# A gated block over 64 sequences: outputs read back by groups, a normalisation ahead of a copy, a wide split ahead of an exponent

## The chip, the cores and the metric

The kernel runs on one core of one Trainium2 chip, in one launch. The time is that of the device in microseconds. Five engines work side by side, each through its own list of instructions, and meet through semaphores: PE (TensorE) multiplies matrices, DVE (VectorE) and POOL (GpSimd) work elementwise on SBUF, DVE on PSUM too, ACT (ScalarE) applies functions, and SP issues DMAs, as ACT does for some.

## The reference

Each of 64 sequences has 256 rows of 512 features, all float32. In short:

```
def xattn(q, k, v, w, b):                    # 16 heads of 32 features
    q, k, v = relu(q), relu(k), relu(v)
    att = softmax(q k^T / sqrt(32))          # 256 x 256 for each head
    return relu(att v @ w.T + b)

def ffn(x, W_r, W_k, W_v, mu_r, mu_k):
    x_prev = x shifted down by one row
    r = sigmoid((mu_r * x + (1 - mu_r) * x_prev) @ W_r)
    k = (mu_k * x + (1 - mu_k) * x_prev) @ W_k
    return r * (relu(k) ** 2 @ W_v)

x = x + tanh(g_xattn) * xattn(layernorm(x), ctx, ctx, w, b)
x = x + tanh(g_ffn) * ffn(layernorm(x), W_r, W_k, W_v, mu_r, mu_k)
```

## The kernel before

**Tiling.** A sequence b has two row tiles u of 128 rows, four feature chunks of 128, and 16 heads n in CH = 4 groups c of GR = 4. Float32 operands of the large products are split into a high and a low part (`q_high`, `k_low`, `o_high`, `o_low`, `xk_high`, `xk_low` and so on), and a product is three matmuls of such parts. ACT makes high parts, DVE or POOL the low ones.

**Attention.** Scores of a head are computed twice. PE makes `scores` (L1084) in one of two banks, `s_bank[n % 2]`; DVE takes each row's maximum, `head_max` (L855). For a group, PE turns the four heads' maxima (L1059), DVE copies them, `copy_m` (L864), and SP moves them by DMA into one row of the stacked queries, `move_m` (L300). PE then makes `shifted_scores` (L1096), in which that row subtracts the maximum, ACT applies `exponent` (L616), and PE sums with the values (L1110) and with ones (L1122, the denominators). For group 1 the denominators come another way: ACT's `sum_exp` (L628) applies the exponential to the first scores of heads 4 to 7 in their bank and accumulates the sum. A later head's `scores` needs the bank back: those of head 7 wait until `sum_exp` of head 5 is done, those of head 10 for `head_max` of head 8.

**Output of attention.** `norm_o` (L877 reciprocal, L879 multiply) writes group c into `o_val[c % 2]`. SP writes it to DRAM, `write_o` (L307), in a transposing layout, and reads a row tile's two groups back as `o_mv` when both are written, `read_o` (L316: 4 DMAs of 64 KB each). ACT copies it out as the high part, `o_high` (L637), POOL makes the low one, `o_low` (L429), and PE projects (L1139, `w_hi,o_hi`). `o_mv` is one buffer, reused by each row tile: it may be overwritten when `o_lo` of the tile before is done. In the kernel before this is guarded by a wait in `norm_o` of the odd groups.

**Second half.** `add_x`, the second layernorm, a turn on PE, the differences between rows (POOL L438) and the mixes `mix_k` (L923) and `mix_r` (L932, four instructions that add to `xd` in place) feed key, value and receptance; `ka_square` (POOL L462) squares the key. `finish` multiplies by the gate (L940: th) and adds to x (L943: x1), which SP stores (L323). `load_x1` on ACT (L534) loads the next x into that buffer, once the store is done.

**Order.** The work is a software pipeline: iteration i holds, interleaved, the first layernorm of sequence i+2, the attention of i and i+1, and the second halves of i-1 to i-3. Each engine has a list of its own for an iteration, written out by hand; iterations -3 to 3 and 60 to 66 are unrolled, the 56 between run as a hardware loop of pairs. Nothing reorders the lists: an instruction that waits holds up all behind it on its engine. The names that follow are those of the rows: `o_hi<-o_mv` is `o_high`, `bank<-bank,m_nat` `sum_exp`, `probs<-bank` `exponent`, `k_raw<-k_raw,k_high` `k_low` (L844, in place), `xk_lo<-xm,xk_hi` `xk_low` (L447), `q_st<-q_dram` `stack_q` (L578, L579), `q_dram<-q_raw` a part of `write_q` (L568), `k_st<-k_dram` `stack_k`.

SP's list of an iteration before, at its start and where tile 0 is read:

```
stack_k(i, 3, par); store(i - 3, 1 - par); move_m(i, 1); write_o(i - 1, 3); read_o(i - 1, 1)
...
load_x(i + 3); move_m(i, 3); write_o(i, 1); stack_k(i + 1, 2, 1 - par); move_m(i + 1, 0); read_o(i, 0)
```

Of the kernel before, what the change touches and what calls it, by code (L numbers as in the profile page):

```python
# [16 lines left out]
def flamingo_block(nc, x, ctx_in, ctx_t, g_xattn, g_ffn, w_t, bias, mu, out):  # L17
# [19 lines left out]
    HD = D // HEADS  # L37
    NU = T // P
# [9 lines left out]
    with es:  # L48
# [119 lines left out]
        o_moved = sem("o_moved")  # L168
# [68 lines left out]
        def _(sp):  # L237
# [71 lines left out]
            def read_o(b, u):  # L309

                if on(b):

                    for half in o_written:
                        sp.wait_ge(half, 16 * (2 * b + u + 1))
                    for m in range(GR):
                        sp.dma_start(o_mv[HD * m:HD * m + HD, :, :],  # L316
                                     o_dram[2 * u:2 * u + 2, :, :, m, :].rearrange("c g f r -> f (c g) r")
                                     ).then_inc(o_moved, 16)
# [12 lines left out]
            def opening(i, par):  # L331
# [6 lines left out]
                elif i == -1:  # L338
                    stack_k(0, 0, 1 - par)
                    stack_k(0, 1, 1 - par)  # L340
                    load_k(1)
                    move_m(0, 0)
                    stack_k(0, 2, 1 - par)
                    load_x(2)
                else:
                    stack_k(0, 3, par)
                    move_m(0, 1)
                    load_w(range(4, 5))
                    write_k(1, 1 - par)
                    move_m(0, 2)  # L350
                    load_w(range(5, 6))
                    keys_written(1)
                    stack_k(1, 0, 1 - par)
                    load_k(2)
                    move_m(0, 3)
                    load_w(range(6, 7))
                    write_o(0, 0)
                    stack_k(1, 1, 1 - par)
                    load_x(3)
                    write_o(0, 1)  # L360
                    stack_k(1, 2, 1 - par)
                    move_m(1, 0)
                    load_w(range(7, 8))
                    read_o(0, 0)
                    write_k(2, par)
                    write_o(0, 2)

            def iteration(i, par):
# [3 lines left out]
                stack_k(i, 3, par)  # L372
                if isinstance(i, int) and i == NB + 2:
                    store_last(i - 3, 1 - par)
                else:
                    store(i - 3, 1 - par)
                move_m(i, 1)
                write_o(i - 1, 3)
                read_o(i - 1, 1)
# [6 lines left out]
                load_x(i + 3)  # L386
                move_m(i, 3)
                write_o(i, 1)
                stack_k(i + 1, 2, 1 - par)
                move_m(i + 1, 0)  # L390
                read_o(i, 0)
# [105 lines left out]
        def _(act):  # L497
# [135 lines left out]
            def o_high(b, u):  # L633
                if on(b):
                    act.wait_ge(o_moved, 16 * GR * (NU * b + u + 1))
# [66 lines left out]
            def iteration(i, par):  # L702
                stack_q(i, 3, par)
                if isinstance(i, int) and i == NB + 1:
                    xr_high(i - 2)
                exponent(i, 0)
                sum_exp(i, 6)
# [72 lines left out]
                exponent(i, 15)  # L780
                sum_exp(i + 1, 5)
                o_high(i, 0)
# [5 lines left out]
        def _(dve):  # L788
# [77 lines left out]
            def norm_o(b, c):  # L866
                if on(b):
# [3 lines left out]
                    if c % 2 == 1:  # L871

                        after(dve, o_lo_ready, NU * b + c // 2)
# [62 lines left out]
            def finish(b, u, par):  # L936
                if on(b):
# [3 lines left out]
                                                   in1=dense_bank[u][:, :], op0=ALU.add, op1=ALU.mult).then_inc(y_ready, 1)  # L941
                    dve.wait_ge(y_ready, NU * b + u + 1)
# [3 lines left out]
            def iteration(i, par):  # L946

                head_max(i, 7)
                halve_gate(i)
                finish(i - 3, 1, 1 - par)  # L950
                copy_m(i, 1)
                norm_o(i - 1, 3)
# [52 lines left out]
                head_max(i + 1, 4)  # L1005
                finish(i - 2, 0, par)
# [363 lines left out]
```

## Time and profile before

| | us |
|---|---|
| median of 3 runs | 2733.62 |
| lowest and highest | 2730.46, 2733.77 |
| profiled execution, its own time | 2731.21 |
| its span | 2729.4 |
| PE busy | 2656.8 (97%) |
| DVE busy | 2298.1 (84%) |
| ACT busy | 1693.1 (62%) |
| POOL busy | 1100.4 (40%) |
| mean granted TensorE clock | 0.988 |

The DMA engines moved 576.74 MB, 211 GB/s over the span. The busy digits of PE are 9 (90% or more) in 37 of the 40 slices; only the first two and the last are below. The share of an engine says how much of the span it computed. With PE at 97%, the time is PE's work and its waits; what another engine does counts only where PE, or something that ends in PE, waits for it. The profiled execution's time is some 1.8 us above its span: what lies around the program.

### The profile page before, as it was taken

How to read it: one execution, taken by the hardware profiler on the slowest of the kernel's cores; microseconds unless marked ns; L12 is line 12 of the kernel's file. 1: busy time of each engine (PE TensorE's matmuls, PEld its weight loads, DVE VectorE, ACT ScalarE, POOL GpSimd, SP SyncE). 2: the span in 40 equal slices, each digit the busy share in tenths (PEclk: the TensorE clock that was granted, in tenths of full speed). 3: DMA queues.
4: the chain of work that ended last, by engine and by line, in shares of the span. 5: the costliest groups of instructions: out<-in, count | busy, mean ns of one | idle time of the engine just before them, and what ended most of it. 6: DMA issues, size and time to landing. Idle time of an engine off the chain costs nothing. (4 is left out here: it accounts for less than half of the span.)

```text
span 2729.4 us, 66171 instructions
## 1 busy us (share of the span) xinstructions
PE 2656.8 (97%) x20354; PEld 2061.7 (76%) x20354; DVE 2298.1 (84%) x4109; ACT 1693.1 (62%) x3531; POOL 1100.4 (40%) x902
## 2 busy tenths in 40 slices
PE   4899999999999999999999999999999999999998
PEld 2677777777777777777777777777777777777776
DVE  6777888888888888888888888888888888888775
ACT  4555666666666666666666666666666666666553
POOL 0243444444444444444444444444444444444434
PEclk9799999999999999999999999999999999999999
DMA  8877778777778778778778778778778778778641
GB/s 252 231 190 213 216 205 231 219 204 231 218 205 231 217 205 233 217 205 233 215 205 235 214 205 235 212 206 237 212 206 236 211 206 234 214 208 232 183 145 45
DMA packets 515023, 576.74 MB, mean 211 GB/s; under 512 B 183072, under 2 KB 414496, under 8 KB 514976
## 3 DMA queue, kind: packets, MB, share of 16 engines
q1 hardware_dynamic: 361456, 340.68, 45.6%
q10 hardware_dynamic: 153520, 235.46, 29.0%
q8 instruction: 26, 0.43, 0.1%
q14 instruction: 21, 0.17, 0.0%
HBM read 373.56 MB, written 201.33 MB: 211 GB/s over the span
## 5 line engine op out<-in xcount | busy, mean ns | idle before, releaser
L616 ACT ACTIVATE probs<-bank 128x512 f32<-128x512 f32 x1024 | 604.2, 596 | 527.8 <-PE bank L1096 477.4
L855 DVE TENSOR_REDUCE m_nat<-bank 128x2 fp32r<-128x512 f32 x1024 | 687.1, 681 | 90.0 <-PE bank L1084 89.8
L1084 PE MATMUL bank<-k_st,q_st 96*128 96x256 f32 x2048 | 439.3, 297 | 18.1 <-ACT bank L628 6.8
L1096 PE MATMUL bank<-q_st,k_st 97*128 97x256 f32 x2048 | 427.0, 290 | 4.9 <-DMA q_st<-m_t 4.5
L1096 PEld LDWEIGHTS bank<-q_st,k_st 97*128 97x128 f32 x2048 | 358.7, 192 | 84.1 <-issue 27.1
L1084 PEld LDWEIGHTS bank<-k_st,q_st 96*128 96x128 f32 x2048 | 360.7, 194 | 81.0 <-ACT bank L628 17.9
L877 DVE RECIPROCAL o_val<-bank 128x256 f32<-128x256 f32 x192 | 336.2, 1751 | 62.6 <-PE bank L1122 59.7
L429 POOL TENSOR_TENSOR o_lo<-o_mv,o_hi 128x512 fp32r<-128x512 f32 x128 | 166.7, 1302 | 444.3 <-ACT o_hi L637 436.1
L628 ACT ACTIVATE bank<-bank,m_nat 128x256 f32<-128x256 f32 x512 | 227.5, 444 | 186.6 <-DVE m_nat L855 186.6
L462 POOL TENSOR_TENSOR xm<-xm 128x512 f32<-128x512 f32 x128 | 133.8, 1045 | 408.0 <-ACT xm L674 408.0
L1139 PE MATMUL bank<-xk_hi,w_hi 128*128 128x256 f32 x1024 | 296.5, 290 | 1.0 <-DVE th L940 1.0
L1139 PE MATMUL bank<-xk_hi,w_lo 128*128 128x256 f32 x1024 | 288.2, 281 | 0.0
L1139 PE MATMUL bank<-xk_lo,w_hi 128*128 128x256 f32 x1024 | 287.9, 281 | 0.0
L1110 PE MATMUL bank<-probs,v_pos 128*32 128x256 f32 x4096 | 278.2, 390 | 0.0
L421 POOL TENSOR_TENSOR rstd<-ve,mhalf 128x1 f32<-128x1 f32 x128 | 69.2, 541 | 456.4 <-DVE ve L907 456.4
L1139 PE MATMUL bank<-w_hi,o_hi 128*128 128x512 f32 x512 | 212.8, 416 | 14.0 <-POOL o_lo L429 13.8
L447 POOL TENSOR_TENSOR xk_lo<-xm,xk_hi 128x512 fp32r<-128x512 f32 x128 | 172.9, 1351 | 128.4 <-DVE xm L923 111.6
L1139 PEld LDWEIGHTS bank<-xk_hi,w_hi 128*128 128x128 f32 x1024 | 192.5, 188 | 27.4 <-issue 25.9
L864 DVE CAST m_t<-bank 8x128 fp32r<-8x128 f32 x256 | 70.9, 277 | 168.6 <-PE bank L1059 168.2
L1139 PE MATMUL bank<-w_hi,ka_hi 128*128 128x512 f32 x512 | 209.1, 408 | 0.0
L1122 PE MATMUL bank<-probs,ones_r 128*32 128x256 f32 x3072 | 209.0, 390 | 0.0
L1139 PE MATMUL bank<-w_hi,xr_hi 128*128 128x512 f32 x512 | 208.0, 406 | 0.0
(94 smaller groups left out, 6088.3 us busy)
## 6 DMA issues: line engine op xcount, KB each, us to landing
q_st<-q_dram ACTq DMA_DIRECT2D x256, 256.0 KB, 4.8
k_st<-k_dram SPq DMA_DIRECT2D x256, 256.0 KB, 4.3
k_raw<-ctx_t_dram SPq DMA_DIRECT2D x256, 128.0 KB, 4.9
q_st<-q_dram ACTq DMA_DIRECT2D x256, 128.0 KB, 2.5
k_st<-k_dram SPq DMA_DIRECT2D x256, 128.0 KB, 4.8
o_dram<-o_val SPq DMA_DIRECT2D x256, 128.0 KB, 2.2
o_mv<-o_dram SPq DMA_DIRECT2D x512, 64.0 KB, 2.1
x<-x_dram ACTq DMA_DIRECT2D x64, 512.0 KB, 6.4
```

What stands on the lines that cost most here:

```text
L429: nc.gpsimd.tensor_tensor(by_tile(o_lo, u), o_mv[:, :, :].rearrange("p g (k a) -> p k g a", k=KC), by_tile(o_hi, u).bitcast(F32), ALU.subt ...
L447: nc.gpsimd.tensor_tensor(xk_lo[:, part, :], xm[:, part, :], xk_hi[:, part, :].bitcast(F32), ALU.subtract).then_inc(xk_lo_ready, 1)
L462: nc.gpsimd.tensor_tensor(part, part, part, ALU.mult).then_inc(ka_ready, 1)
L616: nc.scalar.activation(probs[:, n // GR % 2, n % GR, :, :].rearrange("p v t -> p (v t)"), st_bank[n % 2][:, :], ACT.Exp).then_inc(exp_read ...
L628: last = nc.scalar.activation(scores, scores, ACT.Exp, bias=m_nat[:, SUMMED % 2, g, u:u + 1].bitcast(F32), accum_out=den[:, NU * g + u:NU ...
L855: nc.vector.tensor_reduce(m_nat[:, c % 2, n % GR, :], s_bank[n % 2][:, :].rearrange("p (u y) -> p u y", u=NU), AX_X, ALU.max, negate=True) ...
L877: nc.vector.reciprocal(o_val[:, c % 2, :], pv_bank[:, T:2 * T]).then_inc(rden_ready, 1)
L1084: mm = nc.tensor.matmul(s_bank[n % 2][:, T * u:T * u + T], q_st[0:QK, c, g, P * u:P * u + P], k_st[0:QK, c, g, :], start=True, stop=True)
L1096: mm = nc.tensor.matmul(st_bank[n % 2][:, T * v:T * v + T], k_st[0:ST, c, g, P * v:P * v + P], q_st[0:ST, c, g, :], start=True, stop=True)
L1110: nc.tensor.matmul(pv_bank[HD * g:HD * g + HD, 0:T], v_pos[:, v, HD * h:HD * h + HD], probs[:, c % 2, g, v, :], start=(v == 0), stop=(v == ...
L1122: mm = nc.tensor.matmul(pv_bank[HD * g:HD * g + HD, T:2 * T], ones_r[:, 0:HD].bitcast(F32), moving, start=(n == 0), stop=(n == len(sums) - 1))
L1139: mm = nc.tensor.matmul(dst, lhs[a], rhs[c], start=first and n == 0, stop=last and n == 2, skip_group_check=True)
```

## The change

It has three parts.

- **Reads by halves.** `o_moved` becomes two semaphores. `read_o(b, u, half)` waits for the low part of the tile before (this guard moves here from `norm_o`) and for the write of group 2u + half alone, and reads that group: 4 DMAs of 32 KB for each half. The first half of tile 0 is issued ahead of `move_m(i, 3)`, the second ahead of `move_m(i + 1, 0)` (both stood behind it); the first half of tile 1 stands ahead of the last group's write, the second behind the store. The store itself goes behind that write and `move_m(i, 1)`. `o_high` waits for both halves.
- **DVE.** `finish` becomes `gate` and `finish`. At an iteration's start `gate` and `norm_o` of the last group stand first, then `copy_m`, the rest of the finish, and `mix_r`.
- **ACT.** `o_high(i, 0)` stands ahead of `sum_exp(i + 1, 5)` rather than behind it, and `stack_q(i, 3)` behind `exponent(i, 0)` rather than ahead of it.

```diff
@@ -165,7 +165,7 @@
         rsum_spread = sem("rsum_spread")
         o_ready = sem("o_ready")
         o_written = [sem("o_written0"), sem("o_written1")]
-        o_moved = sem("o_moved")
+        o_moved = [sem("o_moved0"), sem("o_moved1")]
         o_hi_ready = sem("o_hi_ready")
         o_lo_ready = sem("o_lo_ready")
         z_ready = sem("z_ready")
@@ -306,16 +306,15 @@
                     sp.wait_ge(o_ready, CH * b + c + 1)
                     sp.dma_start(o_dram[c].rearrange("g f m r -> (g f) (m r)"), o_val[:, c % 2, :]).then_inc(o_written[c % 2], 16)

-            def read_o(b, u):
-
-                if on(b):
-
-                    for half in o_written:
-                        sp.wait_ge(half, 16 * (2 * b + u + 1))
+            def read_o(b, u, half):
+
+                if on(b):
+                    after(sp, o_lo_ready, NU * b + u)
+                    sp.wait_ge(o_written[half], 16 * (2 * b + u + 1))
                     for m in range(GR):
-                        sp.dma_start(o_mv[HD * m:HD * m + HD, :, :],
-                                     o_dram[2 * u:2 * u + 2, :, :, m, :].rearrange("c g f r -> f (c g) r")
-                                     ).then_inc(o_moved, 16)
+                        sp.dma_start(o_mv[HD * m:HD * m + HD, GR * half:GR * half + GR, :],
+                                     o_dram[2 * u + half, :, :, m, :].rearrange("g f r -> f g r")
+                                     ).then_inc(o_moved[half], 16)

             def store(b, par):
                 if on(b):
@@ -361,7 +360,8 @@
                     stack_k(1, 2, 1 - par)
                     move_m(1, 0)
                     load_w(range(7, 8))
-                    read_o(0, 0)
+                    read_o(0, 0, 0)
+                    read_o(0, 0, 1)
                     write_k(2, par)
                     write_o(0, 2)

@@ -370,13 +370,14 @@
                     opening(i, par)
                     return
                 stack_k(i, 3, par)
+                read_o(i - 1, 1, 0)
+                write_o(i - 1, 3)
+                move_m(i, 1)
                 if isinstance(i, int) and i == NB + 2:
                     store_last(i - 3, 1 - par)
                 else:
                     store(i - 3, 1 - par)
-                move_m(i, 1)
-                write_o(i - 1, 3)
-                read_o(i - 1, 1)
+                read_o(i - 1, 1, 1)
                 keys_written(i + 1)
                 stack_k(i + 1, 0, 1 - par)
                 load_k(i + 2)
@@ -384,11 +385,12 @@
                 write_o(i, 0)
                 stack_k(i + 1, 1, 1 - par)
                 load_x(i + 3)
+                read_o(i, 0, 0)
                 move_m(i, 3)
                 write_o(i, 1)
                 stack_k(i + 1, 2, 1 - par)
+                read_o(i, 0, 1)
                 move_m(i + 1, 0)
-                read_o(i, 0)
                 write_k(i + 2, par)
                 write_o(i, 2)

@@ -632,7 +634,8 @@

             def o_high(b, u):
                 if on(b):
-                    act.wait_ge(o_moved, 16 * GR * (NU * b + u + 1))
+                    for half in o_moved:
+                        act.wait_ge(half, 16 * GR * (NU * b + u + 1))
                     after(act, z_ready, NU * (b - 1) + u + 1)
                     nc.scalar.activation(by_tile(o_hi, u), o_mv[:, :, :].rearrange("p g (k a) -> p k g a", k=KC),
                                          ACT.Copy).then_inc(o_hi_ready, 1)
@@ -700,10 +703,10 @@
                                          scale=0.5).then_inc(th_ready, 1)

             def iteration(i, par):
-                stack_q(i, 3, par)
                 if isinstance(i, int) and i == NB + 1:
                     xr_high(i - 2)
                 exponent(i, 0)
+                stack_q(i, 3, par)
                 sum_exp(i, 6)

                 exponent(i, 1)
@@ -778,8 +781,8 @@
                 load_v(i + 1, 0)

                 exponent(i, 15)
+                o_high(i, 0)
                 sum_exp(i + 1, 5)
-                o_high(i, 0)

             pipeline(act, iteration)

@@ -868,9 +871,6 @@
                     dve.wait_ge(pv_ready, CH * b + c + 1)

                     after(dve, o_written[c % 2], 16 * (2 * b + c // 2))
-                    if c % 2 == 1:
-
-                        after(dve, o_lo_ready, NU * b + c // 2)
                     if c == SUMMED:
                         nc.vector.tensor_copy(o_val[:, c % 2, :], pv_bank[:, T:2 * T]).then_inc(rden_ready, 1)
                     else:
@@ -933,12 +933,15 @@
                                                               in1=xt[:, c, 0:T], op0=ALU.mult, op1=ALU.add)
                     last.then_inc(xr_ready, 1)

-            def finish(b, u, par):
+            def gate(b, u):
                 if on(b):
                     dve.wait_ge(vv_ready, NU * b + u + 1)
                     dve.wait_ge(th_ready, NU * b + u + 1)
                     nc.vector.scalar_tensor_tensor(out=th[:, u, :], in0=th[:, u, :], scalar=1.0,
                                                    in1=dense_bank[u][:, :], op0=ALU.add, op1=ALU.mult).then_inc(y_ready, 1)
+
+            def finish(b, u, par):
+                if on(b):
                     dve.wait_ge(y_ready, NU * b + u + 1)
                     nc.vector.scalar_tensor_tensor(out=x1[:, par, u, :], in0=th[:, u, :], scalar=tgh[:, 0:1],
                                                    in1=x1[:, par, u, :], op0=ALU.mult, op1=ALU.add).then_inc(out_ready, 1)
@@ -947,9 +950,10 @@

                 head_max(i, 7)
                 halve_gate(i)
+                gate(i - 3, 1)
+                norm_o(i - 1, 3)
+                copy_m(i, 1)
                 finish(i - 3, 1, 1 - par)
-                copy_m(i, 1)
-                norm_o(i - 1, 3)
                 if not (isinstance(i, int) and i == NB + 1):
                     mix_r(i - 2)

@@ -1003,6 +1007,7 @@
                 split_low(i, 4, 0)

                 head_max(i + 1, 4)
+                gate(i - 2, 0)
                 finish(i - 2, 0, par)

                 head_max(i + 1, 5)
```

ACT, at the boundary of two iterations inside the loop; `o_hi<-o_mv` is `o_high`, `bank,den<-bank,m_nat` the summed exponents (of head 5 above the branch of iterations, 6 and 7 behind), `q_st<-q_dram` the query stack. Before:

```order
L616 ACTIVATE probs<-bank 128x512
L622 REGISTER_ALU
L628 ACTIVATE bank,den<-bank,m_nat 128x256 x2
L635 ISA
L637 ACTIVATE o_hi<-o_mv 128x4x128
L578 DMA q_st<-q_dram 32x1024
L579 DMA q_st<-q_dram 64x1024
L609 REGISTER_ALU
L206 ISA
L616 ACTIVATE probs<-bank 128x512
```

After, in the same place:

```order
L618 ACTIVATE probs<-bank 128x512
L638 ISA
L640 ACTIVATE o_hi<-o_mv 128x4x128
L624 REGISTER_ALU
L630 ACTIVATE bank,den<-bank,m_nat 128x256 x2
L611 REGISTER_ALU
L206 ISA
L618 ACTIVATE probs<-bank 128x512
L580 DMA q_st<-q_dram 32x1024
L581 DMA q_st<-q_dram 64x1024
```

The high part of the output went ahead of head 5's summed exponent, and the two query DMAs behind the next exponent.

DVE, at the start of an iteration in the loop, behind the maxima of head 7: `th` is the gate, `x` the finish, `m_t` the copy of maxima, `o_val` the normalisation, `xd` the last mix. Before:

```order
L938 ISA
L940 SCALAR_TENSOR_TENSOR th<-th,bank 128x512
L943 SCALAR_TENSOR_TENSOR x<-th,tgh,x 128x512
L861 ISA
L206 ISA
L864 CAST m_t<-bank 8x128
L868 ISA
L206 ISA
L877 RECIPROCAL o_val<-bank 128x256
L879 TENSOR_TENSOR o_val<-bank,o_val 128x256
L932 SCALAR_TENSOR_TENSOR xd<-xd,mu_sb,xt 128x256 x4
```

After:

```order
L938 ISA
L940 SCALAR_TENSOR_TENSOR th<-th,bank 128x512
L871 ISA
L206 ISA
L877 RECIPROCAL o_val<-bank 128x256
L879 TENSOR_TENSOR o_val<-bank,o_val 128x256
L864 ISA
L206 ISA
L867 CAST m_t<-bank 8x128
L946 SCALAR_TENSOR_TENSOR x<-th,tgh,x 128x512
L932 SCALAR_TENSOR_TENSOR xd<-xd,mu_sb,xt 128x256 x4
```

The finish and the copy moved from ahead of the normalisation to behind it.

SP, from the key stack at the start of an iteration in the loop. Before:

```order
L291 DMA k_st<-k_dram 32x1024
L322 ISA
L323 ISA
L323 DMA out_dram<-x 128x2x512
L299 ISA
L300 DMA q_st<-m_t 1x8x128
L306 ISA
L307 DMA o_dram<-o_val 128x256
L314 ISA
L316 DMA o_mv<-o_dram 32x8x64 x4
```

After:

```order
L206 ISA
L313 ISA
L315 DMA o_mv<-o_dram 32x4x64 x4
L306 ISA
L307 DMA o_dram<-o_val 128x256
L299 ISA
L300 DMA q_st<-m_t 1x8x128
L321 ISA
L322 ISA
L322 DMA out_dram<-x 128x2x512
L315 DMA o_mv<-o_dram 32x4x64 x4
```

The write of the last group went ahead of the move of maxima and of the store; one half of the read stands ahead of all three, the other behind them.

## Rows read from the trace of the kernel before

**Rows 1.** Windows: start:end, us, busy of engines, granted clock, DMA share, GB/s

```profile
1319.22:1401.22 82.00, 81.86 (x638) 63.69 (x636) 71.32 (x129) 52.62 (x111) 34.48 (x28) 1.00 0.76 218
1975.22:2015.75 40.53, 40.53 (x319) 31.73 (x318) 34.90 (x65) 25.95 (x55) 17.08 (x14) 1.00 0.76 218
```

**Rows 2.** Timeline, a slow boundary and a quick one: start, us, engine, line, instruction

```profile
1319.38 0.20 ACT L628 ACTIVATION_READ_ACCUMULATOR bank<-bank,m_nat 128x1 f32 x1
1319.97 0.28 PE L1139 MATMUL bank<-xk_hi,w_hi 128*128 128x256 f32 x1
1321.89 0.08 PEld L1059 LDWEIGHTS bank<-ident_r,m_nat 128*8 128x8 f32 x1 [0.52 <-DVE m_nat L855]
...
1975.07 0.21 ACT L628 ACTIVATION_READ_ACCUMULATOR bank<-bank,m_nat 128x1 f32 x1
1975.70 0.28 PE L1139 MATMUL bank<-xk_hi,w_hi 128*128 128x256 f32 x1
```

**Rows 3.** Timeline, `xk_lo` on POOL and the keys on DVE, ahead of either boundary

```profile
1313.57 1.29 POOL L447 TENSOR_TENSOR xk_lo<-xm,xk_hi 128x512 fp32r<-128x512 f32 x1 [0.21 <-issue]
1313.78 2.16 DVE L844 SCALAR_TENSOR_TENSOR k_raw<-k_raw,k_high 128x1024 fp32r<-128x1024 f32 x1
...
1969.70 2.43 POOL L447 TENSOR_TENSOR xk_lo<-xm,xk_hi 128x512 fp32r<-128x512 f32 x1 [0.34 <-issue]
1969.78 1.20 DVE L844 SCALAR_TENSOR_TENSOR k_raw<-k_raw,k_high 128x1024 fp32r<-128x1024 f32 x1
```

**Rows 4.** Groups by line, L844: busy us, mean ns, idle before

```profile
L844 DVE SCALAR_TENSOR_TENSOR k_raw<-k_raw,k_high 128x1024 fp32r<-128x1024 f32 x64 | 125.8, 1966 | 0.0
```

**Rows 5.** Timeline, ACT's DMA issue of `q_raw`, ahead of either boundary

```profile
1312.12 0.53 ACTq L568 DMA_DIRECT2D q_dram<-q_raw  x1
...
1968.12 0.73 ACTq L568 DMA_DIRECT2D q_dram<-q_raw  x1
```

**Rows 6.** Waits, whole span: us in total, times, longest

```profile
PE bank L1139 <- POOL o_lo L429: 13.8, 7, 2.8
```

**Rows 7.** Windows, the longest of the disturbed iterations

```profile
206.01:252.39 46.38, 43.60 (x319) 34.02 (x318) 34.67 (x64) 26.26 (x57) 17.58 (x14) 0.93 0.71 198
```

**Rows 8.** Timeline, ACT, the other `o_high` of an iteration

```profile
1333.83 0.63 ACT L637 ACTIVATE o_hi<-o_mv 128x512 fp32r<-128x512 f32 x1 [1.83 <-DMA o_mv<-o_dram]
1334.37 0.58 ACT L616 ACTIVATE probs<-bank 128x512 f32<-128x512 f32 x1
```

**Rows 9.** Timeline, ACT, the first `o_high` of all

```profile
79.32 0.63 ACT L637 ACTIVATE o_hi<-o_mv 128x512 fp32r<-128x512 f32 x1 [4.43 <-DMA o_mv<-o_dram]
```

**Rows 10.** Timeline, DVE, POOL and PE behind the slow boundary

```profile
1322.47 0.75 DVE L943 SCALAR_TENSOR_TENSOR x<-th,tgh,x 128x512 f32<-128x512 f32 x1
1323.14 0.27 DVE L864 CAST m_t<-bank 8x128 fp32r<-8x128 f32 x1
1325.45 1.67 DVE L932 SCALAR_TENSOR_TENSOR xd<-xd,mu_sb,xt 128x256 f32<-128x256 f32 x4
1327.03 1.28 DVE L855 TENSOR_REDUCE m_nat<-bank 128x2 fp32r<-128x512 f32 x2
1327.36 1.04 POOL L462 TENSOR_TENSOR xm<-xm 128x512 f32<-128x512 f32 x1 [5.91 <-ACT xm L674]
1328.65 0.40 PE L1084 MATMUL bank<-k_st,q_st 96*128 96x256 f32 x2
```

**Rows 11.** Timeline, maxima moved and first used: steady, then in the start-up

```profile
1323.92 0.69 SPq L300 DMA_DIRECT2D q_st<-m_t  x1
1329.60 0.40 PE L1096 MATMUL bank<-q_st,k_st 97*128 97x256 f32 x2
...
43.02 0.69 SPq L300 DMA_DIRECT2D q_st<-m_t  x1
48.06 0.80 PE L1096 MATMUL bank<-q_st,k_st 97*128 97x256 f32 x2 [1.80 <-DMA q_st<-m_t]
```

**Rows 12.** The page, DMA issues: count, KB, us to landing

```profile
o_dram<-o_val SPq DMA_DIRECT2D x256, 128.0 KB, 2.2
```

## The prediction

> **What bounds the kernel now.** I read the windows first. Two stretches from the start of one iteration's first shifted product (sequence i+1, head 0) to a later one: two iterations in 82.00 us, 41.00 each, with PE busy for 81.86; and one of 40.53 us with PE busy for all of it [rows 1]. So PE sets the pace, and the 0.47 us between the two kinds is all that an ordinary iteration loses. The timeline at the boundary shows where. Scores of head 7 wait for ACT's summed exponent of head 5, which ends 0.36 us after the boundary in the slow kind (1319.38 + 0.20) and 0.06 after it in the quick kind; the dense product behind the scores starts at +0.75 and +0.48 [rows 2]. That is 0.27 of the 0.47. The other 0.2 follows at once, at the turn of the maxima, where PE waits for DVE.
>
> Why ACT is late is on DVE and POOL, six microseconds earlier. The scaling of keys (L844) takes 2.16 us where POOL's `xk_lo` record starts 0.21 us before it, and 1.20 us where it starts 0.08 before it; POOL's instruction is then the long one, 2.43 against 1.29 [rows 3]. Only one of the two proceeds at a time. All 64 of them take 125.8 us [rows 4]: with n long ones, 2.16n + 1.20(64 - n) = 125.8 gives 51 long and 13 short. Some 61 boundaries are steady ones, 51 slow and 10 quick. Where POOL's start slips, ACT's issue of `q_raw` took 0.73 us instead of 0.53 [rows 5]; it stands before the `xk_hi` that POOL waits for.
>
> Outside this, PE waits 13.8 us in 7 waits for POOL's `o_lo` [rows 6], in which `o_mv`, read back from DRAM, is late. The iteration with the longest takes 46.38 us at a mean granted clock of 0.93, so that part of it stands at the 1.2 GHz level behind the stall [rows 7]. Against 40.53 it loses 5.85, 2.1 times its wait of 2.8.
>
> **The change, part by part.**
> *`o_high` ahead of the summed exponent of head 5.* From `o_high` to the next ACT instruction is 1334.37 - 1333.83 = 0.54 us [rows 8], and now it stands on the very path that makes PE wait. In a slow iteration the dense product would start at +0.75 + 0.54 = 1.29, against 0.48 with no wait: 0.81 lost, and the second wait, for DVE at the turn, is covered by that. So 40.53 + 0.81 = 41.34, +0.34. In a quick iteration the exponent would end at 0.06 + 0.54 = 0.60; with the 0.39 us that the slow kind needs from its end to the dense product (0.75 - 0.36) that product starts at 0.99, a loss of 0.51: 41.04 us. Ten quick iterations: +5.1. Fifty-one slow ones that stay slow: +17.3; if they turn quick: 51 x 0.04 = +2.0. It also needs `o_mv` 0.6 us sooner, and in the start-up, where `o_high` waited 4.43 us for it with nothing behind [rows 9], the exponents and head 7's scores now wait too: about +3 once (bounds 0 and 4.4).
>
> *Does k_low win the port more often?* The change puts 128 KB of `o_mv` reads, which stood behind the move of the next maxima, ahead of it, so that they are in the queues when ACT issues `q_raw`. The quick kind needs a slip of POOL of only about 0.13 us (0.21 to 0.08), and the issue row moves by 0.20 when it moves [rows 3, 5]. I judge that it turns in 41 of the 51 (nearest rows: 10 of 61 now; bounds 0 and 51). Then 41 x 0.04 + 10 x 0.34 + 5.1 = +10.1 us for this and the part above; bounds +7.1 and +22.4.
>
> *Reads by halves.* Per row tile 256 KB still move, in 8 issues rather than 4 (SP has the idle time: its issues cost nothing on PE). Half 0 needs only group 2u, so it leaves early, and after the last group's write only 128 KB remain. The 7 waits are worth between 13.8 (the waits alone) and 13.8 x 2.1 = 29 us (with the lower clock behind each of them). The two or three short ones had no slow clock worth naming, so I take 24 for all and 20 of it as saved. Against it: in tile 1 the store of x (512 KB) now stands ahead of half 1 in SP's queue, so the saving could be 0.
>
> *DVE's start of the iteration.* Copy of the maxima (0.27) and the second part of the finish (0.75) go behind `norm_o`, which could not have started much earlier: it waits for PE's denominators. Between its multiply and `mix_r`, which started at 1325.45, stand the copy and the finish now: 0.67 from the finish's start to the next (1323.14 - 1322.47) and some 0.2 for the copy, less about 0.13 by which the reciprocal can start sooner than behind both. I take 0.74: `mix_r` at 1326.19. The maximum of head 8, which stood at 1327.03, moves to 1327.77 and ends some 0.65 later at 1328.42, and scores of head 10 on PE, its user, stand at 1328.65 [rows 10]. Slack 0.94 becomes 0.2: cost 0, with nothing to spare. The wait for `o_lo` that leaves `norm_o` cost nothing here, and goes to SP.
>
> *The maxima's move to `q_st`.* It was issued at 1323.92 and used at 1329.60, 5.7 us later. Now the copy ends at about 1325.8 and the issue follows at 1325.9: 3.7 us. One row speaks of it: in the start-up, issue at 43.02, product at 48.06 after a wait of 1.80 for this very move, 5.04 us [rows 11]; 128 KB of `o_dram` land in 2.2 [rows 12]. Bounds 0 and 1.34 us in each iteration. I take 0: the queue of the start-up was full of loads, and 2.2 is the row of the steady loop on that queue.
>
> *The store* leaves 3.5 us later, and with it the next x load on ACT, which is used ten microseconds on: 0, covered by PE. *Query stack behind exponent 0*: it takes off a 0.6 us issue gap before an exponent that PE does not wait for: 0 to -0.1 per iteration; I take 0.
>
> **Sum.** 2731.2 (the profiled execution) + 10.1 + 3 - 20 = 2724.3. The median of the runs shown, 2733.6, is 2.4 above the profiled one: 2726.7, say 2727.
>
> **Rivals.**
> 1. *The port race does not turn.* For it: 51 of 61 go POOL's way now. 2731.2 + 22.4 + 3 - 20 + 2.4 = 2739.0.
> 2. *`mix_r` loses the port to POOL's square* (the slower side). `ka_square` starts at 1327.36 and takes 1.04; `mix_r`'s last of four instructions would start at 1326.19 + 3 x 0.40 = 1327.4, at the same time. If POOL wins, the maximum of head 8 ends about 1 us later, the slack of 0.2 is gone, and PE waits 0.8 us for scores of head 10 in every iteration: 2726.7 + 61 x 0.8 = 2775. It decides from a POOL lead of about 0.1 to 0.2 us. Against it: the lead worked out is 0.0, and a slip of ACT moves POOL back, not forward.
> The Trainium skill, "SBUF — State Buffer", section "Who interferes with whom", says that the pair of ports shared by DVE and GpSimd is an exclusive lock that whoever starts first keeps for a whole instruction; a DVE instruction with two SBUF inputs contends with a reading GpSimd one. By that rule alone POOL, 0.04 ahead, would win here, and this rival would be the forecast. The trace agrees on the lock, but not to the tenth of a microsecond: in [rows 3] POOL's record starts 0.08 first, and it is POOL that waits.
> 3. *The reads of `o_mv` stay late*, dragged by the store ahead of them and the x load beside them: no saving of 20, 2746.7. For it: the store now shares their queue and their moment. Against: half of the bytes are gone by then.
> The Trainium skill, "DMA: Bandwidth & Descriptors", section "Queues, rings and completion order", has each DMA engine take packets of the queues in turns, and within a queue in ring order; by that the half behind the store has 512 KB before it and the x load beside it. No row of before shows that order.
> 4. *The move of maxima is late*: up to 1.34 us x 61, over 2800; half of that is likelier, 2765.
> 5. *More is gained*: all turn, the quicker start of exponent 0 hides half of `o_high`, and all 24 come off: about 2714.
>
> **Chances.** Forecast 0.42, its own range 2718 to 2733; rival 1 0.21; rival 2 0.12; rival 3 0.10; rival 4 0.05; rival 5 0.10. The range 2712 to 2760 leaves out most of rivals 2 and 4. A measurement tells about 0.2% (5.5 us) from no change. Faster (under 2728.1): 0.6 of the forecast and rival 5, 0.25 + 0.10, with a little of rival 1: 0.37. Slower (over 2739.1): half of rival 1, most of 3, all of 2 and 4: 0.11 + 0.08 + 0.17 = 0.36. Same: 0.27.
>
> **What would show it.** The count of long and short L844 (now 51 and 13): mostly short says that the race turned. The dense product at the boundary at about +0.99, and an iteration of 41.0 us where the race turned, 41.3 where not. No wait of PE for `o_lo` in the steady loop, and no iteration near 46 us. A wait of PE (L1084) for DVE's maximum nine microseconds after the boundary means rival 2, one at L1096 for the move of `m_t` rival 4. Wrong altogether if ordinary iterations fall below 40.9: then the 0.54 of `o_high` is not on the path as I have it.

## The result and the profile after

The change makes the kernel slower: 2742.85 us median of 6 runs (2739.48 to 2746.17) against 2732.04 of 6 (2721.71 to 2735.45), a ratio of 1.0046 with a 95% interval of 1.0026 to 1.0066. Forecast was 2727, a gain of 0.25%. The number lies inside the stated range; the sign is the other one. It is rival 1, the race for the port that does not turn, at 2739.0, and 4 us more. One run of e1 and two runs of the kernel before, at 3206, 5066 and 3656 us, were in a slow state and stand in none of the medians and ratios below.

The page after and, below it, the windows of the same 48 iterations before and after (start:end, us, busy time of each engine, granted clock, DMA share, GB/s):

```profile
span 2742.8 us, 66755 instructions
PE 2647.6 (97%) x20354; PEld 2053.6 (75%) x20354; DVE 2305.0 (84%) x4109; ACT 1687.2 (62%) x3531; POOL 1124.4 (41%) x902
```

```profile
376.67:2343.38 1966.71, 1963.67 (x15265) 1528.50 (x15264) 1712.20 (x3073) 1261.72 (x2641) 824.59 (x672) 1.00 0.77 218
```

```profile
372.71:2363.19 1990.48, 1965.43 (x15265) 1529.35 (x15264) 1720.55 (x3073) 1256.66 (x2641) 843.02 (x673) 1.00 0.79 215
```

Divided by 48: 40.97 us an iteration before, 41.47 after. These 48 alone lose 23.8 us. Before them the changed kernel is 4.0 us ahead (372.71 against 376.67), and behind them 6.4 (2742.8 - 2363.19 = 379.6 against 2729.4 - 2343.38 = 386.0). The three add up to the 13.4 by which the spans differ. PE's busy time fell by 9.2 us, from 2656.8. All of that lies outside the 48, where the mean granted clock rose from 0.93 to 0.95 ahead of them and from 0.98 to 1.00 behind; the iteration that took 46.38 us at 0.93 [rows 7] takes 41.88 at 1.00. Inside the 48, PE had no wait to speak of before, and has these now (us in total, times, longest), which are all of the loss:

```profile
PE bank L1089 <- ACT bank L630: 21.1, 48, 0.5
PE bank L1056 <- DVE m_t L867: 3.5, 10, 0.6
```

The ordinary boundary (start, us, engine, line, instruction; in brackets the idle time before it and who ended it):

```profile
1325.61 0.40 PE L1101 MATMUL bank<-q_st,k_st 97*128 97x256 f32 x2
1326.17 0.23 ACT L630 ACTIVATION_READ_ACCUMULATOR bank<-bank,m_nat 128x1 f32 x1
1326.45 0.50 PE L1089 MATMUL bank<-k_st,q_st 96*128 96x256 f32 x2 [0.45 <-ACT bank L630]
1326.79 0.28 PE L1144 MATMUL bank<-xk_hi,w_hi 128*128 128x256 f32 x1
```

The exponent of head 5 ends 0.79 us behind the boundary, where it ended at 0.36 [rows 2], and the dense product starts at +1.18, where it started at 0.75. The race ahead of it, with the four reads of `o_mv` on SP and ACT's issue of `q_raw`, and the group of all 64 key scalings:

```profile
1315.59 1.82 SPq L315 DMA_DIRECT2D o_mv<-o_dram  x4
1318.50 0.53 ACTq L570 DMA_DIRECT2D q_dram<-q_raw  x1
...
1319.97 1.29 POOL L449 TENSOR_TENSOR xk_lo<-xm,xk_hi 128x512 fp32r<-128x512 f32 x1 [0.21 <-issue]
1320.17 2.17 DVE L847 SCALAR_TENSOR_TENSOR k_raw<-k_raw,k_high 128x1024 fp32r<-128x1024 f32 x1
```

```profile
L847 DVE SCALAR_TENSOR_TENSOR k_raw<-k_raw,k_high 128x1024 fp32r<-128x1024 f32 x64 | 130.7, 2042 | 0.0
```

130.7 = 2.16n + 1.20(64 - n) gives 56 long ones, more than the 51 of [rows 4]. The issue takes the 0.53 us of [rows 5]'s slow kind, although the reads issued ahead of it have not landed (the second halves of tile 0 take 3.75 us to land, median of the 48). The waits of PE that the change was to touch (us in total, times, longest):

```profile
PEld bank L1101 <- DMA q_st<-m_t: 7.7, 5, 3.1
PE bank L1101 <- DMA q_st<-m_t: 6.4, 4, 2.8
PE bank L1144 <- POOL o_lo L431: 2.5, 3, 1.6
```

So the waits for `o_lo` fell from 13.8 [rows 6] to 2.5. The maxima's move costs PE four waits, all within the first 114 us; before it had three there, and none later in either kernel. And at the start of an iteration DVE does what was worked out:

```profile
1331.69 0.42 DVE L879 TENSOR_TENSOR o_val<-bank,o_val 128x256 f32<-128x256 f32 x1
1332.03 0.27 DVE L867 CAST m_t<-bank 8x128 fp32r<-8x128 f32 x1
1332.23 0.73 DVE L946 SCALAR_TENSOR_TENSOR x<-th,tgh,x 128x512 f32<-128x512 f32 x1
1332.89 1.66 DVE L932 SCALAR_TENSOR_TENSOR xd<-xd,mu_sb,xt 128x256 f32<-128x256 f32 x4
```

`mix_r` starts at +7.28 from the boundary, where it started at +6.23 [rows 10]. The later boundary has its part in that. In e2 below, whose boundary is that of before, `mix_r` stands at +6.97, 0.74 later, as worked out.

One thing had not been forecast. Of the 48 iterations, 11 take 41.7 to 42.2 us. In one of them (910.83 to 952.54), then in an undisturbed one (828.17 to 869.44), the copy that spreads the inverted sums over `o_val` (L890) and POOL's second square of the key (L464):

```profile
923.48 1.04 POOL L464 TENSOR_TENSOR xm<-xm 128x512 f32<-128x512 f32 x1
923.51 1.16 DVE L890 COPY o_val<-rden 128x256 f32<-128x256 f32 x1
925.19 2.29 DVE L833 TENSOR_SCALAR q_nat<-x_ln,mv,rstd 128x512 f32<-128x512 f32 x2
925.68 1.29 POOL L431 TENSOR_TENSOR o_lo<-o_mv,o_hi 128x512 fp32r<-128x512 f32 x1 [1.16 <-ACT o_hi L640]
...
840.84 1.19 POOL L464 TENSOR_TENSOR xm<-xm 128x512 f32<-128x512 f32 x1
840.84 0.29 DVE L890 COPY o_val<-rden 128x256 f32<-128x256 f32 x1
841.65 1.45 DVE L833 TENSOR_SCALAR q_nat<-x_ln,mv,rstd 128x512 f32<-128x512 f32 x2
```

It is a race of the same kind as that of the keys. Where POOL starts 0.03 us ahead, the copy takes 1.16 us instead of 0.29; q's normalisation comes later by that, meets POOL's `o_lo`, and takes 2.29 for 1.45. The copy of the maxima and the turn of q on PE stand behind them: these are the 10 waits of L1056 above. In all, 27 of the 64 copies are long, where one was before; in the 48 it is 25, and 10 of the 11 iterations above have one. DVE comes to this place 1.05 us later than before (12.79 against 11.74 us behind the boundary, medians of the 48), and so meets an instruction that it used to precede.

### The profile page after: what moved, and what is told of

It is laid out like the page before. It is cut to its first block and busy times, and to the rows that moved or that the text cites. A ratio compares the mean times of both kernels' runs of the same rounds, so it can differ in the third digit from the quotient of the medians.

```text
span 2742.8 us, 66755 instructions
## 1 busy us (share of the span) xinstructions
PE 2647.6 (97%) x20354; PEld 2053.6 (75%) x20354; DVE 2305.0 (84%) x4109; ACT 1687.2 (62%) x3531; POOL 1124.4 (41%) x902
## 5 line engine op out<-in xcount | busy, mean ns | idle before, releaser
L464 POOL TENSOR_TENSOR xm<-xm 128x512 f32<-128x512 f32 x128 | 158.2, 1236 | 475.1 <-ACT xm L677 474.7
L1144 PE MATMUL bank<-w_lo,o_hi 128*128 128x512 f32 x512 | 203.0, 396 | 0.0
```

The costliest lines, as they stand in the source:

```text
L464: nc.gpsimd.tensor_tensor(part, part, part, ALU.mult).then_inc(ka_ready, 1)
L1144: mm = nc.tensor.matmul(dst, lhs[a], rhs[c], start=first and n == 0, stop=last and n == 2, skip_group_check=True)
```

## The experiments

Eleven kernels. Each time is compared with the kernel before, run on the same chip. The ratio is given with each, and gains in us are worked out from it unless medians are named. The last column is the mean of the same 48 iterations in the profile, which is one execution. Executions of the kernel before spread over 15 us (2720.7 to 2736.1 beside e1), so a difference of 0.1 us in that column, 5 us in 48, needs rows beside it.

| kernel | median us | ratio to before (95%) | us an iteration |
|---|---|---|---|
| before | 2727.63 to 2732.04 | 1 | 40.97 |
| the change | 2742.85 | 1.0046 (1.0026, 1.0066) | 41.47 |
| e1 `o_high` first | 2751.94 | 1.0092 (1.0073, 1.0111) | 41.29 |
| e2 change, exponent first | 2720.22 | 0.9971 (0.9960, 0.9983) | 41.18 |
| e3 DVE's order alone | 2876.46 | 1.0545 (1.0527, 1.0564) | 43.74 |
| e11 the same with SP's order | 2744.01 | 1.0051 (1.0035, 1.0067) | 41.57 |
| e4 change, DVE as before | 2735.63 | 1.0028 (1.0016, 1.0039) | 41.33 |
| e7 reads by halves alone | 2717.02 | 0.9962 (0.9949, 0.9975) | 41.07 |
| e10 change, copy before POOL | 2736.84 | 1.0026 (1.0016, 1.0037) | 41.34 |
| e5 before, port to DVE | 2707.42 | 0.9925 (0.9912, 0.9938) | 40.59 |
| e6 change, port to DVE | 2730.15 | 1.0012 (1.0000, 1.0024) | 41.22 |
| e8 reads, port to DVE | 2695.76 | 0.9885 (0.9871, 0.9900) | 40.69 |
| e9 e8 with the query stack moved | 2691.74 | 0.9858 (0.9838, 0.9878) | 40.63 |

**e1: one swap on ACT.**

```diff
                 exponent(i, 15)
-                sum_exp(i + 1, 5)
                 o_high(i, 0)
+                sum_exp(i + 1, 5)
```

> The kernel before with one edit: o_high(i, 0) stands ahead of sum_exp(i + 1, 5). Theory A (this one swap costs the time): +0.37 us in each of some 53 ordinary iterations, as measured between the two traces (40.97 to 41.34), and 3 to 5 us in the start-up: +20 to +25 us, the ordinary iteration at 41.3, L844 still mostly 2.16 us long. Rival B (the cost comes with the DMA order or with DVE's order): within 5 us of the kernel before.

1.0092: 25 us, theory A. (The two profiles lie 19.9 us apart, 15 of them in the 48 iterations: the profiled execution of the kernel before was slower than its median here.) The swap by itself costs more than the whole change, and its boundary is that of the changed kernel, the same wait of 0.45 us, 0.84 us behind the boundary:

```profile
1290.44 0.40 PE L1096 MATMUL bank<-q_st,k_st 97*128 97x256 f32 x2
1291.28 0.50 PE L1084 MATMUL bank<-k_st,q_st 96*128 96x256 f32 x2 [0.45 <-ACT bank L628]
```

**e2: the changed kernel with that swap undone** (the same two lines the other way round).

> The changed kernel with one edit undone: sum_exp(i + 1, 5) stands ahead of o_high(i, 0) again. Theory A: the reads' saving of about 16 us stays and the swap's cost of 20 to 25 goes: 12 to 18 us below the kernel before, ordinary iteration 40.9 to 41.0. Rival B: as the changed kernel, 10 us above before.

0.9971, 8 us below before, where 12 to 18 were expected, and 41.18 us an iteration, where 40.9 to 41.0 were. The swap is the cause of the loss: without it the change gains. Only 4 copies are long here, against 27, so the later boundary has its part in those too; what keeps this kernel from more is in part `o_lo`, for which PE waits 3.2 us in 6 of the 48 iterations.

**e3: DVE's order alone, and e11: with SP's order as well.** e3 takes these lines and leaves SP as it was:

```diff
-                finish(i - 3, 1, 1 - par)
-                copy_m(i, 1)
+                gate(i - 3, 1)
                 norm_o(i - 1, 3)
+                copy_m(i, 1)
+                finish(i - 3, 1, 1 - par)
```

> The kernel before with DVE's order alone: gate, norm_o, copy_m, finish, mix_r at an iteration's start. Theory A (DVE's order is nearly free): 0 to +5 us. Theory C (DVE comes 0.7 us later to the copy of the inverted sums, L890, where POOL's second square of the key holds the shared port; the copy then takes 1.15 us instead of 0.29, and the turn of q on PE waits 0.3 to 0.8 us in some iterations): +5 to +25 us, with long copies in most iterations.

1.0545: 149 us, far outside both theories, and no copy is long, so theory C's mechanism is absent here. I had treated DVE's order and SP's as separate. SP issued in this order, one boundary being at 1297.25:

```profile
1304.43 0.40 SPq L323 DMA_DIRECT2D out_dram<-x  x1
1304.95 0.69 SPq L300 DMA_DIRECT2D q_st<-m_t  x1
1305.69 0.43 SPq L307 DMA_DIRECT2D o_dram<-o_val  x1
1308.89 1.30 SPq L316 DMA_DIRECT2D o_mv<-o_dram  x3
...
1317.16 0.47 PE L1144 MATMUL bank<-w_hi,o_hi 128*128 128x512 f32 x1 [2.05 <-POOL o_lo L429]
```

```profile
PE bank L1144 <- POOL o_lo L429: 98.7, 64, 5.1
PEld bank L1101 <- DMA q_st<-m_t: 21.9, 37, 2.8
PE bank L1101 <- DMA q_st<-m_t: 26.4, 63, 2.6
```

The group's sums are normalised early, but their write stands on SP behind the store, which waits for the finish that now comes last; the write goes out 8.4 us behind the boundary and the read 11.6. PE waits for `o_lo` 64 times. The move of the maxima stands behind the store as well, and PE waits for it 63 times. e11 then gives SP the change's order (write, move, store, then one whole read):

> DVE's new order on the kernel before (which took 1.054 of before's time), and now SP's order with it: the last group's write, the maxima's move, the store, then the read, still in one piece. Theory A (in the 1.054 the write and the read queue on SP behind the store and the move, which wait for DVE): the reads are issued 8.5 us behind the boundary rather than 12, o_low is in time again, within 0.5% of before. Rival (what makes the new DVE order bearable is the reading by halves): still 2% or more above before.

1.0051: most of it is back, so the queue on SP was the cause, theory A (0.5% lies inside the interval). The wait for `o_lo` is still there:

```profile
PE bank L1144 <- POOL o_lo L429: 23.8, 38, 1.7
```

The read stands right behind the store here, and its 64 KB DMAs land 4.75 us after their issue, where they took 2.7 in the kernel before (medians of the 48). With the halves and everything else of the change but ACT's swap, e2, PE waits 5.0 us for `o_lo` instead of 23.8.

**e7: the reads by halves and SP's order alone**, ACT's order and the start of DVE's as before.

> The kernel before with the reads by halves and SP's new order alone; ACT's order and DVE's start as before. Theory A: the waits for o_lo go, -12 to -18 us, ordinary iterations at 40.97 as before, L844 long in at least 45 of 64. Rival: the reads ahead of q_raw's issue turn the port race (L844 short in most), then -30 to -40. Rival D: the maxima's move, behind the write of the last group now, is late for PE: slower than before.

0.9962, 10.4 us less, a little short of theory A. All of the gain lies in the start-up and the end: the 48 iterations lose 0.10 us each on average, which was not expected. The page's DMA rows (KB each, median us from issue to landing), before and after:

```profile
o_mv<-o_dram SPq DMA_DIRECT2D x512, 64.0 KB, 2.1
```

```profile
o_mv<-o_dram SPq DMA_DIRECT2D x1024, 32.0 KB, 3.1
```

These medians mix four places. In the 48 iterations of e7 the first halves land in 1.8 us (tile 1) and 2.2 (tile 0), the second halves in 4.0 and 3.7; the whole reads of before took 2.7 and 2.05. The half of tile 1 that ACT must wait for now stands right behind the store, as the whole read does in e11, and there both are late, with 32 KB at a time as with 64 (4.0 and 4.75 us). Why the second half of tile 0 takes 3.7, with no store ahead of it, is open. So `o_high` of tile 1 starts 14.65 us behind the boundary, where it started at 13.64 (medians). Most iterations bear that: the typical pair is 40.95 and 41.05 us, as against 40.92 and 41.08. Where it starts past 15.1, in 11 of the 48, PE comes to wait for `o_lo`, as here in the iteration that began at 780.51 and took 41.58:

```profile
788.36 0.43 SPq L322 DMA_DIRECT2D out_dram<-x  x1
788.89 2.44 SPq L315 DMA_DIRECT2D o_mv<-o_dram  x4
...
796.05 0.63 ACT L640 ACTIVATE o_hi<-o_mv 128x512 fp32r<-128x512 f32 x1 [2.35 <-DMA o_mv<-o_dram]
...
798.18 0.47 PE L1144 MATMUL bank<-w_hi,o_hi 128*128 128x512 f32 x1 [0.28 <-POOL o_lo L431]
```

The rest of the loss is in the three iterations of 40.53 us that the 48 had before and that e7 has not.

**e4: the changed kernel with DVE's start as before.**

> The changed kernel with DVE's start of the iteration as before (gate, finish, copy_m, norm_o, mix_r); the reads by halves, SP's and ACT's order stay. Theory A: o_high's swap is the cost and DVE's order only adds the long copies L890 (about 6 us): 4 to 8 us below the changed kernel, still 4 to 9 above before; L890 at 0.29 us throughout. Rival (DVE's order is what costs): at or below before by 5 us or more.

2735.63, 7 us below the changed kernel in the median (5 by the ratios, whose intervals overlap) and, by the ratio, 7.6 above before: theory A. No copy is long, an iteration is 0.14 us shorter, and in the 48 iterations PE does not wait for `m_t` at L1056 at all.

**e10: POOL's second square behind DVE's copy.**

```diff
                     pool.wait_ge(kt_relued, 2 * b + half + 1)
+                    if half == 1 and (not isinstance(b, int) or b + 2 < NB):
+                        pool.wait_ge(rsum_spread, b + 3)
```

> The changed kernel with one more wait on POOL: the second square of the key waits until DVE's copy of the inverted sums (L890) is done. Theory A (where POOL comes first there, the copy takes 1.15 us and q's normalisation after it 2.3, and PE waits 0.3 to 0.8 us at the turn of q): no copy over 0.3 us, no iteration of 41.7 or 42 from this place, 4 to 8 us below the changed kernel. Rival (those iterations have another cause, as the loads): no change, they remain.

```profile
POOL xm L466 <- DVE o_val L892: 20.2, 50, 0.4
```

```profile
L892 DVE COPY o_val<-rden 128x256 f32<-128x256 f32 x64 | 18.8, 294 | 7.4
```

The wait holds POOL back 50 times, by up to 0.4 us. All copies are short, the wait of PE for `m_t` is gone, and the iterations take 41.34 instead of 41.47, about what e4 reaches with DVE's old order. The median is 6 us below the changed kernel's, as expected. The two intervals overlap, as with e4; that this race is some 6 us of the loss rests on both kernels agreeing, and on the 3.5 us of waits that go.

**e5 and e6: the race of the keys decided by a wait**, in the kernel before and in the changed one.

```diff
                     after(pool, kt_ready, 2 * b)
+                    if half == 1 and (not isinstance(b, int) or b + 2 < NB):
+                        pool.wait_ge(m_copied, CH * (b + 2) + 1)
```

> The kernel before with one more wait: POOL's xk_low of the second half waits until DVE has copied the maxima of sequence i+1, group 0, so that k_low takes the shared port first. Theory A (the port race in front of the boundary is what separates 41.0 from 40.5 us): L844 1.20 us in all iterations, iterations of 40.5, 51 x 0.47 = 24 us less, 2700 to 2708 us. Rival (the quick iterations have another cause, and the long L844 only goes with it): L844 short, iterations 41.0, no change.

0.9925, 20.5 us less (22.6 between the medians); the median of 2707.42 is in theory A's span, the gain a little under its 24. The reason is that iterations go in pairs, of 40.53 and 40.65 us here (40.92 and 41.08 before): 40.59 is the mean, and the 40.53 of [rows 1] was the shorter of a pair. The rest is as expected, here the key scaling of one iteration and of all, and the 48 iterations' window, in which PE is busy all the time:

```profile
1336.82 1.20 DVE L846 SCALAR_TENSOR_TENSOR k_raw<-k_raw,k_high 128x1024 fp32r<-128x1024 f32 x1
1336.97 2.21 POOL L449 TENSOR_TENSOR xk_lo<-xm,xk_hi 128x512 fp32r<-128x512 f32 x1 [0.57 <-DVE m_t L866]
```

```profile
L846 DVE SCALAR_TENSOR_TENSOR k_raw<-k_raw,k_high 128x1024 fp32r<-128x1024 f32 x64 | 77.0, 1203 | 0.3 <-ACT k_high L607 0.3
```

```profile
368.10:2316.41 1948.31, 1948.31 (x15265) 1525.89 (x15264) 1671.90 (x3072) 1261.38 (x2642) 863.37 (x672) 1.00 0.78 220
```

> The changed kernel with the same wait added. This makes happen what the forecast assumed, the race turned. Theory A: iterations of 41.03 instead of 41.3 to 41.4, L844 1.20 us, the dense product at +0.98: 15 to 20 us below the changed kernel, 0 to 8 below before (the forecast was 2727). Rival (the swap costs more than that on a path of its own): within 5 us of the changed kernel.

e6 makes the forecast's condition true: all 64 scalings short. Its median of 2730.15 is 12.7 below the changed kernel's (9 by the ratios), where 15 to 20 were expected, and by the ratio it is 3 us above before, where 0 to 8 below were. So the swap costs what theory A said for each iteration, but even with the race turned the change gains nothing. The shorter of a pair takes 41.03, as worked out, the other 41.23, and with the iterations that the long copies stretch (21 of 64 are long) the mean is 41.22:

```profile
370.22:2348.62 1978.40, 1964.25 (x15265) 1530.92 (x15264) 1672.44 (x3073) 1263.12 (x2642) 886.45 (x673) 1.00 0.79 217
```

```profile
L892 DVE COPY o_val<-rden 128x256 f32<-128x256 f32 x64 | 36.9, 577 | 7.4
```

**e8 and e9: the parts that gain, together.** e8 is e7 with POOL's wait of e5.

> Reads by halves and SP's order of the changed kernel, ACT's and DVE's order of before, and the same wait on POOL. Theory A: the two gains add, 24 and 10 us: 32 to 38 us below before, about 2692. Rival (they overlap, as the quick iterations bring the reads nearer to where they are needed): 24 or less.

0.9885: 31 us, nearly the sum of 20.5 and 10.4. It is 1 short of theory A's lower end (34 between the medians), and above the rival's 24.

e9 moves the query stack in it:

```diff
-                stack_q(i, 3, par)
                 if isinstance(i, int) and i == NB + 1:
                     xr_high(i - 2)
                 exponent(i, 0)
+                stack_q(i, 3, par)
```

> The kernel with the reads by halves and POOL's wait (which took 0.9885 of before's time), and in it stack_q(i, 3) behind exponent(i, 0). Theory A (that edit is free, PE waits for neither): within 3 us of 0.9885 of before. Rival: exponent 0 comes 0.5 us sooner and takes something off the 0.1 us or so that iterations still stand above 40.53: 3 to 6 us less.

0.9858 against 0.9885: the medians differ by 4 us and an iteration by 0.06 us, which leans to the rival, but the two intervals overlap and the edit's gain is not shown. The ordinary pair is 40.53 and 40.65 us in both kernels; e9 only has fewer iterations above it. At 2691.74 us it is the best version here, 1.4% below before, and 1.9% below the changed kernel.

## Why the prediction was wrong

**What bounds the kernel**: right. PE's own work is the floor (e5: 40.59 us with PE busy all the time), and what stood above it came from the port race (e5). It is 0.38 us rather than 0.47, since 40.53 was the shorter of a pair.

**The swap of `o_high`**: the mechanism and the two prices were right. For a slow boundary 41.34 was worked out; e1 has 41.29, and the changed kernel's undisturbed ones 41.24 to 41.44. For a quick one 41.04 was; e6 has 41.03 and 41.23 in turn. The dense product was put at +1.29 or +0.99; it came at +1.18 and, in e6, +0.98. The start-up's +3: the third boundary comes 4.6 us later (122.10 against 117.53). But e2, which has not the swap, is 4.8 late there and e7 3.1, so most of it does not belong to the swap; by itself (e1) that costs 2.1.

**The step that failed: "I judge that it turns in 41 of the 51".** It turned in none; five more went the other way. The reasoning was that `o_mv`'s reads, issued ahead of `q_raw`, would draw ACT's issue out to 0.73 us as in [rows 5]. That traffic of the SP queue lengthens the issue was taken from two rows that went together, and the traces of the experiments show the opposite. In the five kernels whose reads stand behind the move of the maxima (before, e1, e3, e5, e11), 5 to 10 of the iterations 5 to 59 have an issue of over 0.55 us. In the eight with the halves ahead of it none has, though the reads are on their way at that moment. So the new order on SP took away the very slips that the forecast wanted more of: of the five short scalings that were lost, four are those of iterations 10, 46, 54 and 57, whose issues took 0.69 to 0.85 us before. Why an issue is drawn out in those few stays open.

It was the largest lever in the sum: the turn was worth 12.3 us there (22.4 less 10.1). With the count as it stood, the sum had given 2739.0, the other side of no change. That count was misread as well: "10 quick" took the 13 short scalings less three, but two stand ahead of the first boundary, five in iterations 0 to 4 and two in the unrolled iterations at the end. Only four are in the steady loop, so that ten times 0.51 should have been four times, 2 us and not 5.1. A race that is decided by 0.1 us should have been entered at the count that the trace shows, and there at its place. This step is not the whole of it: e6 has the race turned and still does not come below before. The other two terms that were off are the next two.

**The reads**: 20 were taken, 10.4 measured (e7). The waits for `o_lo` fell from 13.8 us to 4.0. What was missed is a mild form of rival 3: the half behind the store lands late, `o_high` of tile 1 comes 1.0 us later in the median and too late in 11 of the 48 iterations, and the 48 lose 5 us; the start-up loses 3 up to its third boundary.

**DVE's order**: costed at 0. `mix_r` won the port from POOL's first square as forecast, and head 10's scores do not wait (rival 2 did not happen; L464's mean rose from the 1.04 us of [rows 10] to 1.24, which nobody waits for). But I followed the delay to the next user on PE and stopped there. DVE stays late for five more microseconds and meets POOL's second square: 0.13 us an iteration, some 6 us (e4, e10).

**The maxima's move** (rival 4): costed at 0 and right in the steady loop. **The store**: its own delay cost nothing; what stands behind it did, see the reads. **The query stack**: 0 was taken, with 0 to -0.1 as bounds; e9 has -0.06 an iteration, not clear of the noise.

In sum, for an ordinary iteration: swap 0.29 (change less e2), DVE 0.14 (less e4), reads 0.10 (e7), stack -0.06 (e9) make 0.47; measured were 0.50. Each of these is a difference of single executions, and the first holds a part of the second, since 23 of the 27 long copies go with the swap too; the close agreement is in part luck. So is it that the time lies only 16 us above the forecast: the three terms that were off come to 28 (12.3, 9.6 and 6), and smaller ones went the other way (the misread count 3, the swap at 0.29 to 0.32 for 0.34, the stack).

## What to carry to other kernels

An instruction goes ahead of another on a list only if it is needed sooner: here a half-microsecond instruction whose user on PE comes 10 us later was put in front of the one that PE waits for, and that alone cost 0.9%. Where two engines race for a port by tenths of a microsecond, don't hope for the outcome: a single wait on the engine with time to spare fixes it, and was worth 0.75% at no other cost. A median over all DMAs of one kind hides which of them stand behind a store; look at the one that is waited for. And a reordering on one engine is to be read together with the queue that carries its results away: the same DVE order cost 5.5% with SP's old order and 0.5% with the new one.

## What the runs showed of the hardware

- The start of a record does not by itself tell who has the port; each pair of instructions has a threshold of its own. Over the thirteen traces the key scaling lost the port to POOL wherever POOL's record was 0.18 to 0.23 us ahead, and never where it was ahead by 0.16 or less, as by 0.08 in [rows 3]. The copy L890 lost it wherever POOL's record was 0.02 to 0.06 us ahead (0.03 at 923.48 and 923.51), and never where POOL's did not lead.
- A plain copy on DVE from SBUF to SBUF, 128x256, takes part in that race: 0.29 us alone and 1.16 behind POOL. The Trainium skill, "SBUF — State Buffer", section "Who interferes with whom", lists copies among the operations that can take the shared pair in a two-port mode; this case's rows agree, the loser blocked until the other is done.
- A read issued right behind the 512 KB store on the same queue lands late, whatever its size: 4.0 us for 32 KB (e7) and 4.75 for 64 KB (e11), where the same buffer's reads ahead of the store took 1.8 us, and 2.7 when the store was over 4 us away.
- A DMA issue on ACT (`q_raw`) takes 0.53 us in nearly all of the iterations 5 to 59, and in all of them in the eight kernels where 32 KB reads from SP were on their way at that moment; the few of up to 0.96 us came in the kernels whose reads are issued later.
